# Layer 0's ELU as one VectorE operation, with the residual addition on GpSimd

## What is computed

```python
h  = layernorm(x)
Wh = h @ W
e  = (Wh @ a1)[:, :, None] + (Wh @ a2)[:, None, :]
attention = softmax(where(adj > 0, e, NEG_BIG))      # layer 1: leaky relu on e first
x  = x + elu(attention @ Wh)
x  = x + experts(layernorm(x))                       # top 2 of 8
```

## Time and profile before

| | us |
|---|---|
| median of 3 runs | 1315.74 (1313.2 to 1317.15) |
| profiled execution | 1316.0 |
| its span, first to last instruction | 1314.2 |
| TensorE busy | 1061.2 (81%) |
| VectorE busy | 956.5 (73%) |
| GpSimd busy | 706.3 (54%) |
| ScalarE busy | 545.9 (42%) |

### The profile page before, as it was taken

One profiled execution on the slowest core, in us unless ns is written; L12 is line 12 of the kernel. 1 busy time (PEld: TensorE's weight loads), 2 busy tenths in 40 slices (PEclk: granted clock), 3 DMA queues, 4 the chain that ended last, 5 costly groups with the idle time before them and its releaser, 6 DMA issues.

```text
span 1314.2 us, 31672 instructions
## 1 busy us (share of the span) xinstructions
PE 1061.2 (81%) x9392; PEld 888.3 (68%) x9393; DVE 956.5 (73%) x1904; ACT 545.9 (42%) x1223; POOL 706.3 (54%) x752
## 2 busy tenths in 40 slices
PE   6999765369999993477777587579999999899995
PEld 4777554258888883356555373368989987788984
DVE  5888898966777774469899787947766765666673
ACT  3666564912222221577777584112222232122221
POOL 4567657036666653778772281045443206777773
PEclk9999865569999997788879757689999999999998
DMA  9311233025555553336543464447776625444450
GB/s 284 79 49 41 81 113 128 1 65 163 165 161 166 166 160 119 92 104 171 151 137 104 138 200 119 28 131 221 205 223 183 173 78 155 126 136 134 139 144 21
DMA packets 126096, 172.53 MB, mean 131 GB/s; under 512 B 35109, under 2 KB 94000, under 8 KB 125744
## 3 DMA queue, kind: packets, MB, share of 16 engines
q0 software_dynamic: 28288, 83.03, 23.7%
q1 hardware_dynamic: 89504, 88.22, 21.3%
q10 hardware_dynamic: 8208, 0.07, 1.0%
HBM read 100.87 MB, written 71.44 MB: 131 GB/s over the span
## 4 chain that ended last, share of the span: by engine, by line
PE 48%; issue 18%; DVE 12%; POOL 12%; DMA 5%; ACT 3%; POOLq 0%; DVEq 0%; SPq 0%; ACTq 0%
PE bank L970 19%; PE bank L984 18%; POOL WREG L595 5%; PE bank L953 4%; PE bank L781 3%; DVE X L1306 2%; POOL X L678 2%; POOL WREG L643 2%; DMA WREG<-expert_outputs,pos_both 1%; DVE arena L1653 1%; ACT b_bc L1043 1%; DVE stats L1296 1%; DMA out<-X,scatter_row 1%; DMA X<-first_rows,gather_row 1%; DVE arena L1654 1%
## 5 line engine op out<-in xcount | busy, mean ns | idle before, releaser
L1205 ACT ACTIVATE arena<-bank,b1T 128x256 f32<-128x256 f32 (+1 forms) x464 | 176.4, 457 | 507.9 <-PE bank L970 507.8
L984 PE MATMUL bank<-WREG,arena 128*128 x2544 | 301.3, 273 | 16.4 <-issue 11.5
L970 PE MATMUL bank<-arena,WREG 128*128 128x256 f16 (+1 forms) x2784 | 311.7, 266 | 2.6 <-DVE arena L1717 2.6
L984 PEld LDWEIGHTS bank<-WREG,arena 128*128 128x128 f16 x2544 | 245.6, 98 | 53.0 <-issue 23.4
L970 PEld LDWEIGHTS bank<-arena,WREG 128*128 x2784 | 252.5, 99 | 32.2 <-issue 3.6
L1723 DVE CAST arena<-arena 128x1024 f16<-128x1024 f32 (+1 forms) x140 | 82.2, 587 | 192.1 <-ACT arena L1205 192.1
L667 POOL DMA_INDIRECT arena<-split_tokens,gather_row x136 | 134.9, 992 | 124.7 <-DVE gather_row L1694 47.1
L781 PE MATMUL bank<-wg_sb,arena 128*128 128x258 f32 x512 | 145.0, 433 | 47.2 <-ACT arena L1016 39.9
L595 POOL DMA_INDIRECT WREG<-expert_outputs,pos_both x128 | 127.5, 996 | 64.4 <-issue 36.8
L678 POOL DMA_INDIRECT X<-token_rows,gather_row x72 | 73.3, 1018 | 160.6 <-DMA first_rows<-X 67.4
L781 PEld LDWEIGHTS bank<-wg_sb,arena 128*128 128x128 f32 x512 | 105.6, 215 | 71.4 <-ACT arena L1016 41.7
(11 more groups left out here) (204 smaller groups left out, 1497.6 us busy)
## 6 DMA issues: line engine op xcount, KB each, us to landing
first_rows<-X SPq DMA_DIRECT2D x72, 257.0 KB, 4.3
expert_outputs<-arena SPq DMA_DIRECT2D x68, 256.0 KB
X<-in_x SPq DMA_DIRECT2D x16, 512.0 KB, 6.0
split_tokens<-WREG SPq DMA_DIRECT2D x16, 512.0 KB, 2.9
stage_w<-in_L_ffn_W SPq DMA_DIRECT2D x16, 512.0 KB, 4.8
token_rows<-X SPq DMA_DIRECT2D x8, 1024.0 KB, 7.2
token_rows<-WREG SPq DMA_DIRECT2D x16, 512.0 KB, 3.6
stage_w<-in_L_ffn_w SPq DMA_DIRECT2D x16, 256.0 KB, 2.8
```

What stands on the lines that cost most here:

```text
L970: last = mm(hb, w1_at(L, ea, wh, kc, fc), tT[:, tb:tb + width], start=n == 0, stop=n == 3 * KC - 1)
L984: last = mm(ob[a], hsrc[:, h0:h0 + P], w2_at(L, e[a % len(e)], wh, fc), start=fc == 0 and n == 0, stop=fc == FC - 1 and n == 2)
L1205: ins = A(hid[:, h0:h0 + width], bank[2 + 2 * (u % 2) + fc // 2][:, b0:b0 + width], ACT.Gelu if L == 0 else ACT.Relu, bias=cut(b1T, ea * F ...
```

## The change

For layer 0 alone the shift is turned around. The row scaling now adds one, so PSUM holds v + 1; the exponential takes a bias of minus one and still gives exp(v). VectorE does one operation per quarter, in place in `elu_e`: max(min(exp(v), 1), v + 1), which is elu(v) + 1. GpSimd then adds it to `X` (`add_elu`) and signals `x_done`. `X` is thus larger by one throughout, which the layer norm doesn't see, and ScalarE takes the one off again where it forms x plus the normalised tokens, by the bias `nmr` = `nm2` - 1, one small VectorE step more in `token_scales`. The low halves of the first eight pairs of tokens (`low_tokens`, before L643) are written out around the last group's additions.

```diff
+                def add_elu(g, q):
+                    t = g * GT + 2 * q
+                    pool.wait_ge(relu_added[0], at(4 * g + q + 1))
+                    nc.gpsimd.tensor_tensor(xs(t, 2), xs(t, 2), elu_e[q % 2], ALU.add).then_inc(x_done[0], 1)
...
-                    for g in range(1, GROUPS):
-                        diagonal(g)
-                        if g + 1 < GROUPS:
-                            inverse_root(g + 1)
-                        if g + 1 < GROUPS:
-                            no_edges(g + 1)
-                        cut_weights(g - 1, 0)
-                        cut_weights(g - 1, 1)
+                    for g in range(GROUPS):
+                        nxt = g + 1
+                        if g and nxt < GROUPS:
+                            inverse_root(nxt)
+                        if g:
+                            add_elu(g - 1, 3)
+                        if g and nxt < GROUPS:
+                            no_edges(nxt)
+                        if g:
+                            cut_weights(g - 1, 0)
+                            cut_weights(g - 1, 1)
+                        if nxt == GROUPS:
+                            low_tokens(0, 0)
+                            low_tokens(0, 1)
+                        add_elu(g, 0)
+                        add_elu(g, 1)
+                        if nxt < GROUPS:
+                            diagonal(nxt)
+                        else:
+                            low_tokens(0, 2)
+                        add_elu(g, 2)
+                    add_elu(GROUPS - 1, 3)
+                    low_tokens(0, 3)
...
-                  scale=one("rstd", t), bias=minus_one[:]).then_inc(Wh_ev[L], 1)
+                  scale=one("rstd", t), bias=(minus_one if L else plus_one)[:]).then_inc(Wh_ev[L], 1)
...
-                A(elu_e[q % 2], bank[6 + q % 2][:], ACT.Exp, bias=plus_one[:]).then_inc(elu_exp[L], 1)
+                A(elu_e[q % 2], bank[6 + q % 2][:], ACT.Exp, bias=(plus_one if L else minus_one)[:]).then_inc(elu_exp[L], 1)
...
+                last = stt(m, a, -0.5, r, ALU.mult, ALU.mult)
                 if L == 0:
+                    ch.mark(last)
                     ch.mark(ts(one("rstd", first, n), r, 1.0, None, ALU.add))
-                stt(m, a, -0.5, r, ALU.mult, ALU.mult).then_inc(rs2_ready[L], 1)
+                    ch.wait()
+                    last = ts(one("nmr", first, n), m, -1.0, None, ALU.add)
+                last.then_inc(rs2_ready[L], 1)
...
-                stt(xs(t, 2), bank[6 + q % 2][:], -1.0, xs(t, 2), ALU.max, ALU.add).then_inc(relu_added[L], 1)
+                if L == 0:
+                    stt(elu_e[q % 2], elu_e[q % 2], 1.0, bank[6 + q % 2][:], ALU.min, ALU.max).then_inc(relu_added[L], 1)
+                else:
+                    stt(xs(t, 2), bank[6 + q % 2][:], -1.0, xs(t, 2), ALU.max, ALU.add).then_inc(relu_added[L], 1)
```

27 lines of the change are left out of this document (14 added, 13 removed).

## The result

The changed kernel took 1342.43 us (median of 4 runs, 1341.53 to 1346.59), the kernel before 1315.56 us (4 runs, 1313.2 to 1317.15). The ratio is 1.0212, 95% interval 1.0193 to 1.0231: 2.1% slower. The profiled execution took 1341.6 us, of which the span is 1339.8, against 1314.2 before: 25.6 us more. The prediction was 1336.5 us, and 1327 to 1344 its range.

A forecast was written before the change was run, and what follows sets the result against it. A chain of waits through TensorE, ScalarE, VectorE and GpSimd was taken to bound layer 0's 17.08 us rounds. 1316.0 + 12.7 (loop through `diag`) + 6.0 (clock) + 1.9 (end of stage) = 1336.6, rounded to 1336.5 us; range 1327 to 1344.

The forecast's parts named there:

- The loop through diag: Graph rounds: GpSimd's addition ahead of `diag` delays the edge product; round 19.2 us, 2.1 more than 17.08, 12.7 in all.
- The clock: TensorE idle about 2.9 us every round; granted clock falls in four of six rounds: 6 us, ends 0 and 9.
- Rival (1): Graph rounds: same loop through `diag`, but the clock holds: 1330.6 us; chance 0.17.
- The root's loop: Graph rounds: third addition and inverse root come behind `diag`; a round of 18.5 us, hidden below the 19.2.
- Rival (2): Wait for `diag` matters less; root's loop of 18.5 us or GpSimd's 17.9 sets the round: about 1326; chance 0.08.
- The contention: GpSimd slowing VectorE over shared SBUF interfaces in the rounds: left at nothing; at 0.36 us each round, about 1339.
- The wait for elu_e doesn't show: ScalarE's exponentials wait for GpSimd to free `elu_e`, two quarters behind; claimed not to show in these rounds.
- VectorE 3 us less busy per round: Four second additions per round leave VectorE: about 3.1 us per round, busy time 3 us less as a sign.
- GpSimd over 90% busy: Sign in the profile after: GpSimd at over 90% of the round, waiting only for the second maximum.
- The end of the stage: Last group's cuts and addition precede GpSimd's first token difference, 1.7 us late; together 1.9 us, ends 0.5 and 3.5.
- rival (3): Graph rounds and stage end: contention and clock falls in every round, additions at 1.20 + 0.36: 1344 us; chance 0.08.
- Rivals (4) and (5): (4) VectorE's relief sets the round: 1308 us, chance 0.04; (5) no change, the two pull equally: 1316, chance 0.03.

The follow-up runs named there:

- the kernel with the wait filled: Changed kernel plus three extra 128x512 products on TensorE just ahead of layer 0's edge product, filling its wait for `diag`; ratio 1.0083.
- e6_cuts_first: Changed kernel with the last group's two weight cuts ahead of the addition of the previous group's last quarter; ratio 1.0152.

## Why the prediction was right, and where it was not

The mechanism was the predicted one, and the time lies in the range, 6 us above the forecast. By its steps:

- **The loop through diag.** Right, and to 0.01 us: the edge product comes 12.70 us behind the second-pair project, 12.69 was worked out (78.36 - 65.67). That is partly luck: the addition is 1.26 us and not 1.13, outside its ends of 1.06 and 1.20, but `diag` begins 0.05 before it ends, and the exponential came 0.1 earlier. At full clock this way gives 19.1 us with the changed kernel's 12.70 and the 6.40 of the edge product's way back (6.56 was given), and 19.2 in the kernel with the wait filled.
- **The clock.** The falls came in six rounds of six, not four. From the edge product to the project are 7.84 to 8.10 us instead of 6.40, so a fall costs 1.4 to 1.7 us there, as the 1.5 said, and six of them 9.6, above the end of 9. Taking the falls away gained only 7.5 (124.13 - 116.68), or 1.2 a round, since the root's loop then holds the round at 19.47. Rival (1), no falls at all, is out for this kernel.
- **The root's loop.** "It hides below the 19.2" is true of the changed kernel: ScalarE's next scaling waits for TensorE and not for the root. Its size is wrong: 18.5 us were given. In the changed kernel the root's last step ends at 135.52, and with the hand-over of 0.04 and the 0.71 to the project the loop is 19.4 us; it shows as the 19.47 of the kernel with the wait filled, and with `diag` first it is 19.2. The third addition does not follow `diag` at once but waits 1.10 us for the third maximum. Putting `diag` first therefore won nothing in the rounds, and over six rounds 14.3 us are left at full clock instead of 12.7. Rival (2), where this loop was to give 1326, was priced by the same number and falls with it. (Its 1326 lay just below the stated range, whose low end was reckoned with 2.4 us for the end of the stage where the rival had 1.9.)
- **The contention.** This is the step that failed: "I have left that at nothing", for the small steps had "1.7 us of slack". Held, L1362 and L1365 took 1.80 us longer than 0.17 each, and GpSimd waited. In the changed kernel that is hidden behind the wait for `diag` and the falls of the clock; it costs as soon as either is mended. The trace of before had rows that would have told it, and they were not read. This is VectorE and GpSimd of the kernel before at the end of the stage:

```profile
142.70 0.21 DVE L1286 SCALAR_TENSOR_TENSOR cols<-cols 128x48 f32<-128x48 f32 x1 [0.24 <-DVE cols L1284]
142.94 0.95 DVE L1288 SCALAR_TENSOR_TENSOR cols<-cols 128x48 f32<-128x48 f32 x1
```

```profile
142.74 1.09 POOL L585 TENSOR_TENSOR b_bc<-stacked_id,arena 128x512 f32<-128x512 f32 x1 [1.29 <-ACT arena L1027]
```

  The second of two like steps takes 0.95 instead of 0.21 us and ends at 143.89, with `diag` (143.83). The row of 1.05 us in rows 5, from which the surcharge of 0.36 us came, is of another kind. It stands beside this instruction of GpSimd:

```profile
81.96 1.49 POOL L579 TENSOR_SCALAR no_edge<-b_bc 128x512 uint8<-128x512 int32 x1
```

  That ends at 83.45, and VectorE's addition had ended at 83.11, 0.34 us sooner. A surcharge read beside an instruction with one tensor as its input did not carry over to one with two.
- **The maximum costs nothing more.** Right: L1420 takes 0.68 or 0.69 us, also beside additions on GpSimd.
- **The wait for elu_e doesn't show.** Right in the changed kernel, where the third exponential waits for TensorE; wrong as soon as `diag` goes first (1.47 us).
- **VectorE 3 us less busy per round.** Only 1.0 less, since 1.8 us of held steps count as busy. Without additions it is 3.0 less (15.24 to 12.23), so 3.1 was a sound price for what was taken away.
- **GpSimd over 90% busy.** No: 17.19 of 20.58, or 84%, for the round had become longer than its work and it also waits for the third maximum.
- **The end of the stage.** 4.5 us instead of 1.9, above its end of 3.5. Of the parts, the softmax was given 1.0 late and is 2.6: the edge product comes 2.0 us later behind two additions (2.49 us), and the way from it to the softmax is 0.6 longer, with products at the lower clock both before (1.92 us for two) and now (2.07); the first token transposition was given 1.7 late and is 4.1. The cuts' place is 2.1 of it, by their own experiment; the rest was not taken apart.
- **What was not in the sum.** The 2.2 us ahead of the rounds come and go. `e6_cuts_first` runs the same program up to the last group, and this is the first edge product of the changed kernel, then that of `e6_cuts_first`:

```profile
26.76 2.05 PE L816 MATMUL bank<-b_bc,same_graph 128*128 128x512 f32 x2 [3.13 <-issue]
...
26.82 1.10 PE L818 MATMUL bank<-b_bc,same_graph 128*128 128x512 f32 x2 [2.96 <-issue]
```

  Behind it the granted clock was 0.50 from 27 to 30 us in the first and 1.00 in the second, and the first project of a first pair follows 4.77 and 3.08 us later (3.08 before as well). So 1.7 of the 2.2 us are a fall of the clock there, which one execution has and another hasn't. The -2.8 behind the stage was not foreseen, and its cause is open.

Of the 5.1 us between 1336.5 and the profiled 1341.6, 3.1 are the rounds (1.6 what is left at full clock, which the root's loop sets, and 1.5 what the falls add), 2.6 the end of the stage, 2.2 the start and -2.8 the part behind the stage. The median of 1342.43 lies nearer to rival (3) with its 1344 than to the forecast, and that is no proof of it: its falls in every round did occur, its price for contention was not what made the changed kernel slow. Rivals (4) and (5), faster and unchanged, are out.

The idea itself could bring little from the first. By the stage's rows the run without additions puts the whole prize at 7 us, or 0.5% (its ratio, on another chip, says 0.8 to 1.6%), and no way of dividing the additions that was tried reached even the time of before: behind the root the queue of GpSimd is full, with held steps in it (two additions), or VectorE's separate additions hold the root (one).

## What to carry to other kernels

Before moving work to an idle engine, remove it altogether in a run: that gives the ceiling, here 0.9 us of 17.1 a round, and the ceiling was smaller than any of the new costs. Look at what stands behind the moved step in the new engine's queue, and count a gap on TensorE at more than its length if its clock is seen to fall behind such gaps. Taking one cost away gives only the distance to the next loop, so read again what the engine waits for afterwards. When products are added to keep TensorE busy, see that they don't become the bound themselves, and read whether two engines' instructions end together before calling a long one slow.

## What the runs showed of the hardware

- **A small step beside an instruction of the other engine with two tensors in SBUF as inputs lasted until that one ended.** On VectorE a step of 0.17 us took 1.16 us beside a 1.26 us addition on GpSimd and 0.98 beside the 1.06 us `diag`; with the addition halved (0.73 us) 0.59. On GpSimd steps of 0.20 us took 0.51 to 0.74 beside VectorE's additions and subtraction of 0.69. VectorE's maximum, which reads one operand from PSUM, and its statistics were not held. The Trainium skill says on its page "SBUF — State Buffer", section "Who interferes with whom", that a VectorE instruction with two SBUF inputs contends with a GpSimd instruction that reads SBUF, and that the later of the two is blocked until the first is done. For these the trace agrees: VectorE's held steps ended 0.01 to 0.06 us behind the other's end, GpSimd's 0.05 to 0.07. One of the held steps, L1365 with 0.98 us, has a single tensor as its input; the page names a two-port mode of such instructions as a second case, and no run here shows in which mode it was.
- **Beside a 1.49 us GpSimd instruction with one tensor as input the block was shorter.** An addition of VectorE with two SBUF inputs that began 0.1 us behind the mask's start ended 1.15 us behind that start, 0.34 before the mask's end, in all six rounds of the kernel before (82.06 to 83.11 against 81.96 to 83.45). One that began 0.7 us behind the start of such an instruction took its usual 0.69 (84.10 against 83.42). There the trace does not bear out a block until the end. A VectorE step with one tensor as input did last until the end there too: at 19.96 in the kernel before, 0.29 us instead of 0.17, beside an instruction from 18.72 to 20.22, while the two-input steps at 19.47, 19.56 and 19.76 took their 0.17.
- **In the rounds a gap of 2.76 to 3.40 us on TensorE brought the granted clock down each time**, 6 of 6 in the changed kernel: from 1.00 to 0.50, the 1.2 GHz level, between 0.5 us ahead of the gap's end and 1.1 behind it, for some 3 us. (So it was in all 27 such gaps, of five executions.) A fall made TensorE's way from the edge product to the project 1.4 to 1.7 us longer; without the falls the round was 1.2 us shorter there and 1.6 where they were at the project. Gaps of 1.15 to 1.39 us (one addition behind the root) and 1.65 us (two) left the clock at 1.00 in every round. The length of the gap alone does not decide it: ahead of the first edge product a gap of 2.96 to 3.02 us left the clock at 1.00 in five executions (`e6_cuts_first` above is one), and a gap of 2.68 to 3.13 brought it down in seven others.
- **An f32 addition of 128x512 on GpSimd** took 1.26 us (1.28 on the mean of 32), of 128x256 0.73; VectorE's took 0.69 for 128x512.
